# Attention passes of a graph network: six groups of selections, 52 places, and ScalarE's copies and requests in another order

## What is computed

```python
q = (h @ Wq + bq).reshape(n, HEADS, C)
k = (h @ Wk + bk).reshape(n, HEADS, C)
v = (h @ Wv + bv).reshape(n, HEADS, C)
e = (edge_attr @ We).reshape(-1, HEADS, C)
k_j = k[src] + e
alpha = jnp.einsum('ehc,ehc->eh', q[tgt], k_j) / jnp.sqrt(jnp.float32(C))
amax = jax.ops.segment_max(alpha, tgt, num_segments=n)
ex = jnp.exp(alpha - amax[tgt])
denom = jax.ops.segment_sum(ex, tgt, num_segments=n)
a = ex / denom[tgt]
msg = (v[src] + e) * a[..., None]
out = jax.ops.segment_sum(msg, tgt, num_segments=n).reshape(n, HID)
```

## Time and profile before

| | |
|---|---|
| median of 3 runs | 8843.98 us (8842.91 to 8860.0) |
| profiled execution, its own time | 8843.59 us |
| its span | 8841.8 us |
| GpSimd busy | 6279.9 us (71%) |
| TensorE busy | 5227.1 us (59%) |
| VectorE busy | 3721.5 us (42%) |
| ScalarE busy | 3199.8 us (36%) |
| DMA, mean | 181 GB/s |

### The profile page before, as it was taken

One profiled execution on the slowest core, in us unless ns is written; L12 is line 12 of the kernel. 1 busy time (PEld: TensorE's weight loads), 2 busy tenths in 40 slices (PEclk: granted clock), 3 DMA queues, 4 the chain that ended last, 5 costly groups with the idle time before them and its releaser, 6 DMA issues. The chain is left out here.

```text
span 8841.8 us, 130681 instructions
## 1 busy us (share of the span) xinstructions
PE 5227.1 (59%) x25255; PEld 4453.3 (50%) x25255; DVE 3721.5 (42%) x10780; ACT 3199.8 (36%) x13039; POOL 6279.9 (71%) x6563
## 2 busy tenths in 40 slices
PE   2556555557555555554666666666676666666666
PEld 2445444445444444443555555555555555555553
DVE  4000000002000000003677777777787777777778
ACT  4555555553333333332322222222222222222222
POOL 4777777773777777776677777777557777777776
PEclk7766677778555555556777777777787777777777
DMA  5555555556444444445667767676646766677663
GB/s 177 177 176 172 174 178 177 177 175 226 125 122 122 122 122 123 122 125 157 200 211 217 220 208 217 210 214 214 190 135 209 217 214 214 213 219 216 213 218 107
DMA packets 748040, 1597.27 MB, mean 181 GB/s; under 512 B 194927, under 2 KB 402184, under 8 KB 727292
## 3 DMA queue, kind: packets, MB, share of 16 engines
q10 hardware_dynamic: 344768, 846.48, 28.5%
q0 software_dynamic: 249536, 614.81, 24.7%
q1 hardware_dynamic: 152956, 127.62, 4.7%
HBM read 1268.68 MB, written 319.67 MB: 180 GB/s over the span
## 5 line engine op out<-in xcount | busy, mean ns | idle before, releaser
L1739 POOL DMA_INDIRECT conv_held<-key_value,conv_src x3128 | 3002.4, 960 | 1204.4 <-issue 929.3
L2092 ACT ACTIVATE conv_kv<-conv_held 128x256 f32 x3320 | 1090.6, 403 | 2554.1 <-PE conv_ps_sums L1979 1442.4
L890 POOL DMA_INDIRECT second_msg<-sage_hidden_projected,second_src x1516 | 1430.3, 943 | 587.4 <-issue 459.0
L890 POOL DMA_INDIRECT first_msg<-sage_in,first_src x1564 | 1475.6, 943 | 499.3 <-issue 475.8
L1979 PE MATMUL conv_ps_sums<-conv_kv,conv_sel 128*128 128x136 f32 x6640 | 1380.0, 365 | 545.7 <-DVE sums L1889 517.1
L1964 PE MATMUL conv_ps_query<-query_table,conv_selT 128*128 x6640 | 1236.4, 344 | 563.0 <-DMA conv_selT<-selections_turned 426.9
L1979 PEld LDWEIGHTS conv_ps_sums<-conv_kv,conv_sel 128*128 128x128 f32 x6640 | 1194.5, 257 | 704.7 <-DVE sums L1889 528.3
L1964 PEld LDWEIGHTS conv_ps_query<-query_table,conv_selT 128*128 128x128 f32 x6640 | 1087.1, 245 | 642.2 <-issue 640.0
L1108 PE MATMUL second_ps_sums<-second_msg,second_sel 128*128 x3328 | 828.3, 429 | 797.9 <-ACTq L960 796.9
L1108 PE MATMUL first_ps_sums<-first_msg,first_sel 128*128 x3328 | 705.8, 377 | 877.1 <-ACTq L960 869.6
L1889 DVE TENSOR_TENSOR sums<-sums,conv_ps_sums 128x136 f32 x3320 | 970.5, 292 | 572.5 <-DVE sums L1889 220.4
(11 more groups left out here) (270 smaller groups left out, 4534.7 us busy)
## 6 DMA issues: line engine op xcount, KB each, us to landing
conv_selT<-selections_turned ACTq DMA_DIRECT2D x414, 512.0 KB
conv_sel<-selections ACTq DMA_DIRECT2D x414, 512.0 KB
selections<-first_sel ACTq DMA_DIRECT2D x52, 2048.0 KB
selections_turned<-first_selT ACTq DMA_DIRECT2D x416, 256.0 KB
second_sel<-selections ACTq DMA_DIRECT2D x104, 1024.0 KB, 5.2
conv_held<-key_value,conv_src POOLq DMA_INDIRECT x3128
first_msg<-sage_in,first_src POOLq DMA_INDIRECT x1564, 2.7
second_msg<-sage_hidden_projected,second_src POOLq DMA_INDIRECT x1516
```

The costliest lines, as they stand in the source:

```text
L890: pool.indirect_dma_start(msg[:, to * MW:to * MW + D], None, table, bass.IndirectOffsetOnAxis(ap=src[:, lap % 2, j:j + 1], axis=0)).then_i ...
L1739: pool.indirect_dma_start(held[:, (g * GR + i) % HELD, :], None, t.kv_d, bass.IndirectOffsetOnAxis(ap=src[:, lap % 2, j:j + 1], axis=0)).t ...
L2092: last = act.activation(kv[:, place_of_step(c * CH + j), :], held[:, bass.ds(from_tiles[j % (CH // 2)], 1), :].rearrange("p a d -> p (a d) ...
```

## The change

- `sel` has six groups (SELS) in place of four, with three semaphores in place of two. A request for the groups n and n + 1 (counted through the pass) waits for the sums of the groups up to n - 5, where it waited for those up to n - 3, and it may stand further ahead.
- The ring `kv` has 52 places in place of 56.
- ScalarE's order within a stage: copy 1 goes ahead of the two exponentials, right behind copy 0; the registers of the copies are loaded in a step of their own (`tiles_of`), for copies 4 to 7 ahead of copy 3 and for copies 0 to 3 of the next chunk ahead of copy 7; of chunk b's four selection requests, the first two are made in the stage before (around copy 7), the third between copies 2 and 3, the fourth ahead of copy 4; the lists are requested ahead of copy 5.

The diff:

```diff
-PLACES = 56
+PLACES = 52
...
+SELS = 6
...
-        sel = sb("sel", [P, SELG, GR, P])
+        sel = sb("sel", [P, SELS, GR, P])
...
-        sel_in, selT_in = ([sem(f"{k}{q}") for q in range(SELG // 2)] for k in ("sel_in", "selT_in"))
+        sel_in, selT_in = ([sem(f"{k}{q}") for q in range(n // 2)] for k, n in (("sel_in", SELS), ("selT_in", SELG)))
...
-                                pe.wait_ge(sel_in[k // 2 % (SELG // 2)], 16 * ((KG * c + k) // SELG) + 16)
+                                pe.wait_ge(sel_in[(KG * c + k) // 2 % (SELS // 2)], 16 * ((KG * c + k) // SELS) + 16)
...
-                            last = pe.matmul(sums_of(h, step), sel[:, k % SELG, step % GR, :],
+                            last = pe.matmul(sums_of(h, step), sel[:, (KG * c + k) % SELS, step % GR, :],
...
-                    half = q % (SELG // 2)
-                    act.wait_ge(sums_ready, KP * c + 2 * (2 * q + 1) + 2 + 2 * KP - 2 * SELG)
-                    act.dma_start(sel[:, 2 * half:2 * half + hi - lo, :, :].rearrange("p k i w -> p (k i w)"),
+                    n = KG * c + lo
+                    at = n % SELS
+                    if n >= SELS:
+                        act.wait_ge(sums_ready, 2 * (n + 2 - SELS) + 2 * KP)
+                    act.dma_start(sel[:, at:at + hi - lo, :, :].rearrange("p k i w -> p (k i w)"),
...
-                from_tiles = []
+                from_tiles = {}
+
+                def tiles_of(a, half):
+
+                    c, h, g = a
+                    if half == 0:
+                        act.wait_ge(list_in[h], 16 * g + 16)
+                    regs = [act.alloc_register(f"{tag}_held{c}_{half}_{i}") for i in range(CH // 2)]
+                    act.load(regs, lists[0:1, h, half * (CH // 2):(half + 1) * (CH // 2)])
+                    from_tiles[half] = [act.snap(r, donate=True, min_val=0, max_val=HELD - 1) for r in regs]
...
-                    select(b, 0)
-                    select(b, 1)
                     if a is not None:
                         select_turned(a, 1)
                         copy(a, 0)
+                        copy(a, 1)
...
                     if a is not None:
                         select_turned(a, 2)
-                        copy(a, 1)
                         copy(a, 2)
+                    select(b, 2)
+                    if a is not None:
+                        tiles_of(a, 1)
                         copy(a, 3)
                     if after is not None:
                         weights(after)
                     if a is not None:
                         select_turned(a, 3)
-                    select(b, 2)
+                    select(b, 3)
                     if a is not None:
                         copy(a, 4)
-                        copy(a, 5)
-                    select(b, 3)
                     if after is not None:
                         lists_of(after)
+                    if a is not None:
+                        copy(a, 5)
+                    if after is not None:
                         records(after)
                     if a is not None:
                         copy(a, 6)
                     if following is not None:
                         select_turned(following, 0)
-                    if a is not None and groups(a) == KG:
-                        copy(a, 7)
+                    if a is not None:
+                        select(a, 0)
+                    if following is not None:
+                        tiles_of(following, 0)
+                    if a is not None:
+                        if groups(a) == KG:
+                            copy(a, 7)
+                        select(a, 1)
```

More of the change, by code:

```diff
@@ L2042, in select @@
                     lo, hi = 2 * q, min(2 * q + 2, groups(b))
-                    half = q % (SELG // 2)
-                    act.wait_ge(sums_ready, KP * c + 2 * (2 * q + 1) + 2 + 2 * KP - 2 * SELG)
-                    act.dma_start(sel[:, 2 * half:2 * half + hi - lo, :, :].rearrange("p k i w -> p (k i w)"),
+                    n = KG * c + lo
[3 more added lines that the diff above has]
+                    act.dma_start(sel[:, at:at + hi - lo, :, :].rearrange("p k i w -> p (k i w)"),
                                   t.sel_d[bass.ds(c, 1), :, lo * GR * P:hi * GR * P]
-                                  .rearrange("a p w -> p (a w)")).then_inc(sel_in[half], 16)
+                                  .rearrange("a p w -> p (a w)")).then_inc(sel_in[at // 2], 16)
                 def select_turned(a, q):
@@ L2079, in copy @@
                     n = KG * c + k
[L2080 to L2085, removed]
                     tiles = act.value_load(lists[0:1, h, CH + k:CH + k + 1], min_val=1, max_val=GROUPS)
@@ L2092, in copy @@
                         last = act.activation(kv[:, place_of_step(c * CH + j), :],
-                                              held[:, bass.ds(from_tiles[j % (CH // 2)], 1), :].rearrange("p a d -> p (a d)"), ACT.Copy)
+                                              held[:, bass.ds(from_tiles[j // (CH // 2)][j % (CH // 2)], 1), :].rearrange("p a d -> p (a d)"), ACT.Copy)
                     last.then_inc(copied, 1)
@@ L2138, in _ @@
                 select_turned(first, 1)
+                tiles_of(first, 0)
+                tiles_of(first, 1)
                 copy(first, 0)
@@ L2150, in _ @@
                 select_turned(chunk(0, 1), 0)
+                select(first, 0)
+                select(first, 1)
                 copy(first, 6)
+                tiles_of(chunk(0, 1), 0)
                 copy(first, 7)
```

## The result

The changed kernel took 8786.9 us (median of four runs, 8777.1 to 8794.4) against 8844.0 us (four runs, 8842.9 to 8860.0): a ratio of 0.9935, interval 0.9921 to 0.9949. It is faster by 0.65%; forecast were 8,781 us.

The account below looks back on a forecast made before the run. GpSimd's gathers at 1.25 us each were taken to bound 95% of both attention passes. Holds -76, requests +15, tail -3, places +1 made -63 us from 8843.6: 8781 us; ends -105 to -10 (8739 to 8834), 8-in-10 range 8730 to 8840.

Parts of the forecast that it names:

- Holds, -76 of 95: GpSimd's idle time waiting for held places that ScalarE's copies free: 95 us in both passes, four fifths to go, -76 us.
- second sign: SPq L1712 and the issue excess fall from 95 to about 20; landing entries stay or grow by some 15.
- Places (1) and (2): Holds at copy 1 behind the two exponentials and copy 4 behind a selection request and register load; both to go wholly.
- Place (3): Hold at copy 6 behind the records; moves only by VectorE's 1.1 us and stays in part.
- Requests, +15: The moved selection request makes a second, smaller cluster that delays gathers' landings: 15 us, bounds 0 and 62 us.
- Tail, -3: After the last gather VectorE waits 1.44 us for TensorE behind the last two requests; requesting ahead saves 3 us.
- Chain 39.1 -> 37.5 us: Time per stage from one fac exponential to the next falls by 1.1 and 0.5, just under the gathers' 38.6.
- A: Rival: the holds only move, the copy-6 hold takes over; 6 us gained, 8838; 10%.
- B: Rival: more than the holds, half of the landing waits go too; 8733; 9%.
- C: Rival: the moved request, between copies 2 and 3, starves gathers, 1.2 us a stage or 125 us; slower, 8891; 9%.
- D: Rival: half of C, 0.6 us per stage, 62 us; 8828, no measurable change; 6%.
- E: Rival: fac's exponential held behind a late tile, 2 us in every stage, priced at +104 us; 1%.

Follow-up runs that it names:

- e7: The changed kernel, but SP instead of GpSimd waits for the gathers' landing and tells ScalarE, seeing group g + 3 landed before releasing g + 1: 8859.7 us, 1.0027.
- e17: The changed kernel with a stage's requests spread, 20 held and 48 step places, and SP telling of landings in the order of e13: 8682.2 us, 0.9829.
- e13: The changed kernel with SP telling of landed gathers, waiting for landing g + 2 only behind release g: 8737.5 us, 0.9889.
- e12: The changed kernel with registers of copies 0 to 3 loaded behind a stage's last request, ahead of copy 0, not ahead of copy 7: 8831.1 us, 0.9993.

## Why the prediction was right, step by step

8,781 us were forecast and 8,786.9 measured (8,777.1 profiled). The mechanism is the one forecast, fewer holds in front of a queue that sets the rate. That the number came within 6 us is luck: four sizes of the sum were off, and they cancelled: the holds brought 26 us less than worked out and the tail nothing, but the requests cost 19 us less and the long gathers, not counted at all, brought 10. The low end of the range's working, -105, does not follow from its terms either: all 95 us of holds, 3 for the tail, 1 back for the places and nothing for the requests make -97, 8747.

- *The gathers' rate is the bound.* Held in every kernel. First to last start was to fall to about 2,025 each; it fell to 2,026.8 and 2,022.3. With every hold and landing wait taken away the passes come to 1,972, 1% above 1.25 us a gather.
- *Holds, -76 of 95: mis-sized at both ends, -50.* The 95 us took all "issue" time above 0.30 us for holds. By row, 74.2 are holds; 13.1 are idle inside a group, which nothing on ScalarE can end, and some 7 stand between groups without a copy that had just ended. By the prediction's own way of counting the fall is 108.2 to 59.3, 49 us, not the 75 of its second sign. Places (1) and (2) went wholly, as worked out. Place (3), the copy behind the records, kept 23.9 of 35.0 us; of 74 us two thirds went, not four fifths. That holds stay at copy 6 was also named as a sign of being wrong, and that much of it came. The row that the prediction read for this place was read wrongly: the four activations from 5075.09 to 5076.60 are the last two of copy 6, which ended at 5075.79, and the first two of copy 7. The hold is copy 6's all the same; the gather follows its end by 0.81 us, as with the others.
- *Requests, +15: -4 in the whole change.* But the term is a difference of two large ones that I had not seen: closer requests at the stage's end cost 59 us (123.3 against 63.9), and the load of 16 registers between them gives 53 to 69 us back (112.6 against 59.7, 123.3 against 53.9). I priced that load at nothing, and the place that I looked at, behind the moved third request, was the one that costs nothing.
- *Long gathers, 0: -10.* Not forecast. In every kernel but e7 (47.3) they are less than the 46.6 of before, 28.7 to 41.2 us, in the slower ones too; no run says why.
- *Tail, -3: +0.7.* From the last gather's start to the last sum added took 37.9 and 37.7 us, now 38.1 and 38.2. Earlier requests did not shorten it, so the wait for TensorE at the end was not for them.
- *52 places, +1.* The line counts 160 as said, from 148, and its busy time goes from 35.7 to 37.3 us, 1.6 us more:

```profile
L1867 DVE COPY conv_kv<-conv_ps_small 128x128 f32<-128x128 f32 (+7 forms) x160 | 37.3, 233 | 1.5 <-PE conv_ps_small L2000 1.5
```

  No wait shows in the trace for it, and the places were not tried alone.
- *Chain 39.1 -> 37.5 us.* From one fac exponential to the next it is 39.0 us on the mean of the changed kernel's first pass (39.6 before), with the gathers' stops in it; in the stage shown 5036.84 - 4995.53 = 41.31, in which copies 0 and 1 again waited for tiles (4.60). The chain was not the bound: in e17 all engines run a stage in 1,972.3 / 52 = 37.9 us.
- *VectorE's wait before its multiply, down by a third.* On copies it fell by half, from 410.4 us, but the wait only took other names in part:

```profile
L1764 DVE TENSOR_TENSOR conv_kv<-conv_ps_query,conv_kv x830: 625/683/693, 4287.5 to 8572.0; 128x512 f32<-128x512 f32 x166
...
  ACT conv_kv L2098: 206.4, 106
  PE conv_ps_query L1965: 142.1, 128
  issue: 104.4, 76
```

  In sum 452.9 us against 516.8: 64 us less, about the length of the gain. VectorE's work is the same, so its idle time falls by what the passes lose; its other waits were not split.

Of the rivals, **A** (holds only move) is nearest to what the loads alone do: 0.9992, with copy 6's hold up from 35.0 to 40.5, though copies 1 and 4 lost more than that. **B** did not come, since landings did not fall by half; e13 and e17 show what it would have been worth. **C**, starved gathers, is real and was placed wrongly: not in the second, smaller cluster but at the stage's end, where it costs the requests alone 59 us and the changed kernel nothing, thanks to a load that stands between. Its price, 125 us, was twice too high, and its condition (0.75 us a stage) was not reached: 59 / 104 = 0.57. **D** was just this size, and e12 is a kernel of its time, 8831.1 measured, 8828 worked out, but by requests that stand close at the stage's end, not by the moved third one. **E** did not come at a price: in 33 of 104 stages fac starts more than 0.5 us after drop, held by the copy ahead of it (2.55 us is its wait for drop in the stage above, where it is not), in 6 of them more than 2 us; but VectorE's idle time in front of facm is 2.7 us in the whole run, as before, so the delay is hidden as worked out. Its price was also added up wrongly: 2 us in each of 104 stages are 208 us, not 104.

## What to carry to other kernels

Where one queue issues small gathers at a fixed rate and all else hides behind it, first write that rate times the count beside the stage: the difference is all that any re-ordering can win, and it should be read row by row, since a hold and an idle without a named cause share one entry. Don't let the issuing queue wait for its own landings only to tell others; give that to an engine which waits anyway, in the order in which the events come, for one group too far ahead turned a gain of 0.46% over the changed kernel into a loss of 0.92%. And when large requests of another queue move, look at what stands between them: their closeness to each other cost more than their earlier start brought.

## What the runs showed of the hardware that I had not expected

- A gather of 128 rows lands late when several 512 KB requests of another queue begin close together: with four within 2.8 us the landing waits were 123 and 113 us for two passes (requests alone, e12), with four spread over 3.35 to 3.9 us 54 to 68 in seven kernels. The requests carry the same bytes in all; their positions differ.
- GpSimd's queue had idle time inside groups, always between a group's first and second gather, in all kernels where it waits for landings itself (10.7 to 18.6 us), and 2 to 11 us between groups where nothing is named. When SP did the waiting there was 0.9 us inside groups in e13 and in e17, and nothing unnamed between groups; but in e7, where SP also waited, but late, 25.8 us stood inside groups. No run shows what it is.
- One load of 16 registers on a sequencer's queue, some 1.1 us long (the gap in which it stands is 2.60 us with it and 1.54 without), moved behind the next copy and two requests, changed the run by 0.58%, through the requests on either side of it and not by its own time.
